# One fused transformer layer: who multiplies the Mamba sums by their gate, and when the experts' rows are added

## The reference, cut to what matters

```python
x = L0_attn_x                                   # (8, 512, 256)
xn = _layernorm(x)
x = x + attention(xn) + experts(xn)             # experts: 16, capacity 320, gathered by slot
xn = _layernorm(x)
x = x + mamba(xn) + quantised_linear(xn)

def mamba(h):                                   # 512 channels, 16 states
    x, z = split(h @ in_proj_w.T)
    u = silu(causal_conv(x) + conv1d_b)
    dt_low, B, C = split(u @ x_proj_w.T)
    delta = softplus(dt_low @ dt_proj_w.T + dt_proj_b)
    # h_t = exp(delta * A) * h_(t-1) + delta * B * u ;  y_t = sum over states of C * h_t
    y = scan(...) + u * D_param
    return (y * silu(z)) @ out_proj_w.T
```

## Time and profile before

| | |
|---|---|
| median of 3 executions | 2026.71 us (2022.96 to 2026.82) |
| the profiled execution | 2028.68 us, its span 2026.9 us |
| TensorE's mean granted clock | 0.864 |
| busy over the span: PE, DVE, ACT, POOL | 1669.0, 1511.9, 998.1, 892.4 us |
| Mix loop, first to last scan | 1075.6 to 2014.7 us |

### The profile page before, as it was taken

How to read it: one execution, slowest core, us unless ns; L and a number is a source line. 1 busy time by engine, 2 the same in 40 slices (tenths; PEclk the granted TensorE clock), 3 DMA queues, 4 the chain that set the end, 5 groups by cost and what they waited for, 6 DMA issues and landing times. The chain is left out here.

```text
span 2026.9 us, 22043 instructions
## 1 busy us (share of the span) xinstructions
PE 1669.0 (82%) x6616; PEld 747.4 (37%) x6616; DVE 1511.9 (75%) x2254; ACT 998.1 (49%) x1524; POOL 892.4 (44%) x662
## 2 busy tenths in 40 slices
PE   7388999999999999999987678687886869878465
PEld 7252534536253443526233123233332323323032
DVE  6446474564646466454658999999999999999998
ACT  3115435252533435253565756656575665657542
POOL 2710000000000000000349787978788887877863
PEclk9988989899898989999879677898877788887666
DMA  5573451536364351626234232433424233341520
GB/s 192 197 117 106 78 147 43 89 108 104 105 93 131 58 121 66 105 98 107 88 110 168 104 116 95 129 118 119 145 84 157 95 125 109 119 147 54 166 94 11
DMA packets 103331, 223.83 MB, mean 110 GB/s; under 512 B 12913, under 2 KB 65266, under 8 KB 99554
## 3 DMA queue, kind: packets, MB, share of 16 engines
q1 hardware_dynamic: 100194, 214.70, 38.2%
q0 software_dynamic: 3072, 8.37, 1.3%
HBM read 169.57 MB, written 53.48 MB: 110 GB/s over the span
## 5 line engine op out<-in xcount | busy, mean ns | idle before, releaser
L1325 POOL TENSOR_TENSOR work<-rep,bc 128x1024 f32<-128x1024 f32 x256 | 596.4, 2355 | 152.8 <-PE ps L1657 144.3
L1554 DVE TENSOR_TENSOR_SCAN ps<-ps,work 128x512 f32<-128x512 f32 x512 | 624.0, 1219 | 14.1 <-POOL work L1325 8.3
L1447 ACT ACTIVATE ps<-rep,a_neg 128x512 f32<-128x512 f32 x512 | 344.9, 688 | 294.2 <-DVE work L1560 292.2
L832 DVE TENSOR_REDUCE m<-ps 128x1 f32<-128x512 f32 x512 | 328.1, 685 | 164.0 <-PE ps L967 160.4
L719 ACT ACTIVATE prob<-ps 128x1024 f32<-128x1024 f32 x256 | 257.5, 1021 | 233.2 <-PE ps L991 231.4
L1560 DVE TENSOR_TENSOR work<-ps,bc 128x512 f32<-128x512 f32 x512 | 344.2, 672 | 0.0
L637 POOL TENSOR_TENSOR m_parts<-m,nil 128x16 bf16<-128x16 f32 x32 | 7.0, 220 | 590.0 <-DVE m L832 590.0
L1632 PE MATMUL ps<-xn_sb,front_w 128*128 128x512 f32 (+1 forms) x448 | 214.4, 632 | 33.3 <-ACT xn_sb L1381 33.3
L1657 PE MATMUL ps<-work,pick 128*32 128x512 f32 x1024 | 163.5, 717 | 83.5 <-DVE work L1560 83.5
L967 PE MATMUL ps<-k_st,q_st 96*128 96x512 bf16 x512 | 202.3, 439 | 35.6 <-DVE m L832 25.4
L991 PE MATMUL ps<-q_st,k_st 99*128 99x512 bf16 x512 | 166.5, 423 | 0.9 <-DVE e_rest L808 0.4
(11 more groups left out here) (206 smaller groups left out, 2004.2 us busy)
## 6 DMA issues: line engine op xcount, KB each, us to landing
rep<-rep_rows SPq DMA_DIRECT2D x128, 512.0 KB, 6.3
front_w<-in_w SPq DMA_DIRECT2D x32, 1024.0 KB, 8.5
bc<-bc_rows SPq DMA_DIRECT2D x32, 512.0 KB, 4.7
rep_rows<-inputs SPq DMA_DIRECT2D x32, 512.0 KB, 5.4
qk_parts<-parts SPq DMA_DIRECT2D x96, 128.0 KB
q_st<-qk_parts SPq DMA_DIRECT2D x96, 128.0 KB, 10.1
k_st<-qk_parts SPq DMA_DIRECT2D x96, 128.0 KB, 11.5
dispatch<-zeros SPq DMA_DIRECT2D x4, 1280.0 KB, 10.6
```

Source lines behind the costliest of these rows:

```text
L832: nc.vector.tensor_reduce(m[:, g % 2, qt, 2 * pair + i:2 * pair + i + 1], ps[:, S0 + i, :], AX.X, ALU.max).then_inc(s_reduced, 1)
L1325: nc.gpsimd.tensor_tensor(work[:, n % WS, :, :], rep[:, g % RS, 2 * h:2 * h + 2, 1, :], bc[:, k, 0, :].unsqueeze(1).broadcast_to([P, 2, SE ...
L1447: nc.scalar.activation(state(m), rep[:, g % RS, 2 * h + i, 0, :], ACT.Exp, scale=a_neg[:, c, 2 * h + i, k:k + 1]).then_inc(decay_ready, 1)
L1554: nc.vector.tensor_tensor_scan(state(m), state(m), work[:, n % WS, i, :], 0.0, ALU.mult, ALU.add).then_inc(state_ready, 1)
```

## The change

- On VectorE `gate_y` is left for the last sequence alone (`gate_last`). For the other 28 chunks ScalarE copies the bank into a new buffer `y_rows` (one place, `YS = 1`) behind the decays of the fifth piece of the next chunk (`take_y`, `GATE_ACT = 4`), and GpSimd multiplies it into `sz` behind its drive of 12 pieces after the chunk (`gate_y`, `GATE_POOL = 12`).
- `seed` waits for ScalarE's copy (`y_taken`), the out-projection for GpSimd's product (`gated`). ScalarE's next copy waits for the product before it.
- The weighting of the experts' rows moves from piece 21 to piece 17 on ScalarE, the addition from 26 to 24 on GpSimd, the scaling of the input from 25..28 to 26..29.

```diff
+GATE_ACT, GATE_POOL = 4, 12
+YS = 1
...
-ACT_AT = {"weigh": -11, "normalise": -3, ...
+ACT_AT = {"weigh": -15, "normalise": -3, ...
...
-POOL_AT = {"gather": -16, "add": -6, "root": -1, "down": 7, "up": 10, "input": 25}
+POOL_AT = {"gather": -16, "add": -8, "root": -1, "down": 7, "up": 10, "input": 26}
...
+        y_rows = buf("y_rows", [P, YS, SEQ])
...
+                def gate_y(b, c):
+                    pool.wait_ge(y_taken, b * DC + c + 1)
+                    if b:
+                        pool.wait_ge(sz_ready, b)
+                    else:
+                        pool.wait_ge(z_taken, DC)
+                    nc.gpsimd.tensor_tensor(sz[:, b % 2, c, :], y_rows[:, (b * DC + c) % YS, :], sz[:, b % 2, c, :], ALU.mult).then_inc(gated, 1)
...
                     drive(n // PIECES, n % PIECES)
+                    if n >= GATE_POOL + PER_CHUNK and (n - GATE_POOL) % PER_CHUNK == 0:
+                        c = (n - GATE_POOL) // PER_CHUNK - 1
+                        if c // DC < BATCH - 1:
+                            gate_y(c // DC, c % DC)
...
+                def take_y(b, c):
+                    act.wait_ge(summed, (b * PIECES + (c + 1) * PER_CHUNK) // 2)
+                    if b * DC + c >= YS:
+                        act.wait_ge(gated, b * DC + c - YS + 1)
+                    nc.scalar.activation(y_rows[:, (b * DC + c) % YS, :], ps[:, YB, :], ACT.Copy).then_inc(y_taken, 1)
...
                     decay(b, q)
+                    if n >= GATE_ACT + PER_CHUNK and (n - GATE_ACT) % PER_CHUNK == 0:
+                        c = (n - GATE_ACT) // PER_CHUNK - 1
+                        if c // DC < BATCH - 1:
+                            take_y(c // DC, c % DC)
...
-                        gate_y(c // DC, c % DC)
+                        if c // DC == BATCH - 1:
+                            gate_last(c % DC)
...
                 def seed(b, c):
-                    if c or b:
-                        pe.wait_ge(y_ready, b * DC + c)
+                    if b == BATCH - 1 and c:
+                        pe.wait_ge(y_ready, c)
+                    elif b or c:
+                        pe.wait_ge(y_taken, b * DC + c)
...
-                                pe.wait_ge(y_ready, b * DC)
+                                pe.wait_ge(gated, b * DC)
```

More of the change, by code:

```diff
@@ L72 @@
 GATE = 2
+GATE_ACT, GATE_POOL = 4, 12
+YS = 1
 PE_AT = {"turn_x": (-2, -2), "x": (0, 2, 4, 6), "turn_quant": (9, 9), "bc": 12, "dt": (14, 14, 16, 16), "z": (23, 24, 26, 27)}
-ACT_AT = {"weigh": -11, "normalise": -3, "turned": (0, 0), "x": (4, 6, 8, 10), "round": 5, "silu_u": 11, "quant": (12, 12), "rows": 14,
+ACT_AT = {"weigh": -15, "normalise": -3, "turned": (0, 0), "x": (4, 6, 8, 10), "round": 5, "silu_u": 11, "quant": (12, 12), "rows": 14,
           "dt": (16, 16, 18, 18), "softplus": 20, "z": (26, 27, 29, 30), "silu_z": 31}
 DVE_AT = {"max": 0, "statistics": -8}
-POOL_AT = {"gather": -16, "add": -6, "root": -1, "down": 7, "up": 10, "input": 25}
+POOL_AT = {"gather": -16, "add": -8, "root": -1, "down": 7, "up": 10, "input": 26}
 OUT_PROJ, OUT_COPY = (18, 19, 20, 21), (22, 24)
@@ L1172, in mix_block @@
         summed = sem("summed")
+        y_taken = sem("y_taken")
+        gated = sem("gated")
         y_ready = sem("y_ready")
@@ L1560, in read, with gate_last @@
                     nc.vector.tensor_tensor(work[:, n % WS, i, :], state(m), bc[:, k, 1, :], ALU.mult).then_inc(read_ready, 1)
-                def gate_y(b, c):
+                def gate_last(c):
+                    b = BATCH - 1
                     dve.wait_ge(summed, (b * PIECES + (c + 1) * PER_CHUNK) // 2)
[L1564 to L1567, removed]
+                    dve.wait_ge(sz_ready, b)
                     nc.vector.tensor_tensor(sz[:, b % 2, c, :], ps[:, YB, :], sz[:, b % 2, c, :], ALU.mult).then_inc(y_ready, 1)
@@ L1613, in _ @@
                 read(2 * BATCH * PIECES - 1)
-                gate_y(BATCH - 1, DC - 1)
+                gate_last(DC - 1)
             @block.tensor
@@ L1729, in _ @@
                                 pe.wait_ge(out_copied, b * HALVES)
-                            pe.wait_ge(y_ready, b * DC + 2)
+                            pe.wait_ge(y_ready, 2)
                             if t % 2 == 0:
@@ L1735, in _ @@
                         if b == BATCH - 1 and q == LAST_GATED[t]:
-                            pe.wait_ge(y_ready, b * DC + 3)
+                            pe.wait_ge(y_ready, 3)
                             out_gated(b, t, TB[t // 2], range(2, 3))
@@ L1783, in _ @@
                 sum_states(BATCH * PIECES // 2 - 1)
-                pe.wait_ge(y_ready, BATCH * DC)
+                pe.wait_ge(y_ready, DC)
                 for t in range(TT):
```

## The result

The changed kernel takes 2075.23 us (median of 4, 2072.5 to 2076.19) against 2026.03 us (median of 4, one more than in the table before the change): 2.44% slower, ratio 1.0244, interval 1.0230 to 1.0258. I had forecast 2056 us, its own range 2046 to 2066 and the wide one 2034 to 2072. The sign and the chain of waits came as forecast, the size did not: +49 us instead of +29.

What follows compares the result with a forecast made beforehand. The prediction took a loop through GpSimd's root, not VectorE, as the bound: 3.0 + 2.2 = 5.2 us a period, 26 over five, + 5 - 2.4 = +29, so 2056 us; own range 2046 to 2066, wide 2034 to 2072.

Steps and rivals of the forecast that it cites:

- the loop from A to A: Path through TensorE, ScalarE and GpSimd back to ScalarE's normalisation; claimed to set the period, 119.4 us growing to about 124.6.
- A: Moment when ScalarE's normalisation, after waiting about 3.3 us for GpSimd's shift and rstd, can start, once per period.
- The statistics' wait: VectorE's 2.2 us wait for GpSimd's experts' addition; to vanish, 11.0 us in five periods, but costed at nothing.
- GpSimd's stretch from piece 24 to A: GpSimd's nearly gapless work from the drive of piece 24 to the root; to grow by 2.2 us per period.
- The seed is 6.6 us late behind the silu: TensorE's seed of chunk 1 waits for ScalarE's copy of piece 12; GpSimd's drive of piece 16 begins 6.8 us later.
- The last gather lands 2.8 us later: Rows arrive 2.8 us after the last issue; ScalarE waits 3.2 us before weighting, delaying dt's second half 3.0 us.
- slow landing: Rival, chance 0.12: gathers fall on the rep loads and take 7.1 us, giving 2082 us; half of that, 2069.
- The sum: Total of the terms: 5.2 us a period, 26 over five, 5 before the first A, -2.4 after the last: +29.
- Gather in time: Rival, chance 0.15: weighting finds its rows, only GpSimd's 2.2 us per transition remain, +11, 2038 us.
- VectorE sets the pace: Rival, chance 0.09: A follows VectorE, so its savings of 16.8 to 28 us count; 2010 to 1999 us.
- The port lock: Rival, chance 0.04: a gate on GpSimd waits for a VectorE scan of 1.2 us; +7, 2063 us.
- No effect: Rival, chance 0.05: the late sum costs only what VectorE gave, time within 0.2%.

Runs made afterwards that it cites:

- e4: The kernel before with only the moves (weighting behind piece 17, addition behind 24, input scalings from 26), all gates on VectorE: 2030.50 us.
- e8: The kernel before with the addition behind piece 24 and the root behind GpSimd's drive of piece 29 instead of 31: 2021.25 us.
- e12: The kernel before, gates on VectorE, with the moves, the root behind piece 28 and the maxima scaled by ScalarE: 2004.00 us.
- e2: The changed kernel with ScalarE's copy one piece earlier (GATE_ACT 3), in front of the silu of u: 2043.31 us.
- e3: The changed kernel with ScalarE's copy in front of the silu and the weighting back behind piece 21: 2048.48 us.
- e6: The changed kernel with the four gathers issued behind the drives of pieces 12 and 13 instead of 16 and 17: 2046.14 us.
- e10: The changed kernel with ScalarE's copy in front of the silu and the root behind GpSimd's drive and gate of piece 28 instead of 31: 2003.00 us.
- e5: The changed kernel with the three moves taken back (weighting 21, addition 26, input scalings from 25), the gates' new path alone: 2046.94 us.
- e9: The changed kernel with half the bytes of chunk 3's rep load, which runs while the gathers land, left out: 2067.20 us.
- e11: The changed kernel with the copy in front of the silu, the root behind piece 28 and the maxima scaled by ScalarE: 1998.22 us.

## Why the forecast was right and where it failed

*The pace is set by the loop from A to A, and VectorE's savings are worth nothing.* Right. The statistics' wait went and nothing came for it (e4); in the change VectorE waits 6.89 us at piece 30 (4 to 6 forecast). With the root taken out of the way the same savings count (e8, e12: the period becomes VectorE's own work).

*GpSimd's stretch from piece 24 to A is 38.0 us instead of 35.8.* Right: 1445.85 - 1407.81 = 38.0. It is 38.1 in e2, e3 and e6 too, where it is what remains, with a drive of piece 24 that comes 0.7 to 1.3 us later than before; with the root moved out of it (e10) the loss is gone.

*The seed is 6.6 us late behind the silu.* Right in its cause (e2), and nearly in size. In the period shown it is 7.4 us late; the other 0.8 us are TensorE's start on x, eight matmuls in 6.51 us instead of 5.68. In three of the five periods they take 5.7 to 5.8 us and the seed starts 55.7 to 55.8 us after A, as forecast. Over the five it is 7.05 us late in the mean.

*The last gather lands 2.8 us later.* This is the step that failed, a term mis-sized: the rows came 6.45 us after the last issue (6.0 in the mean of five). ScalarE waited 5.3 us, not 3.2, although it reached piece 17 2.1 us later than before, which I had not counted; dt's second half slipped by 7.2 us (6.3 in the mean) instead of 3.0. I took the median of 24 gathers, although the slide by 6.8 us put the last two of each four behind the issue of the load of chunk 3. I had named that as a rival ("slow landing"), gave it 0.12, and ended the range just above its half case. That case, 2069 us, and the full one, 2082, enclose the result. e6, e5 and e9 show the contention. The warning stood in the trace of before: the one gather that took 7.1 us is the only one there that was issued just behind a load of rep, by 0.6 us (1128.64 and 1128.06), and the last of the four, which decides, took 3.1 to 4.4 us in the five other sequences.

*The sum.* In the period shown: seed and its start 0.8 more than forecast, landing 3.6 more, and 1.0 less because the out-projection and seed of piece 18 went faster once begun (8.67 us from its start to the drive of piece 24 instead of 9.70). That is about 3.2 more, 8.4 against 5.2. In the mean of the five it is 3.05 more a period, 8.25 against 5.2: 0.5 from the late issue, 3.2 from the landing, and some 0.5 less behind it. Before the first A it is 7.1 instead of 5, after the last -0.9 instead of -2.4.

*The rivals.* "Gather in time" is e2 and e6: 2043 and 2046, not 2038, because piece 24 comes at A + 84.3 and A + 84.9 there instead of A + 83.6. "VectorE sets the pace" is out for this kernel (e4). The port lock on the gates is out: GpSimd's gates took 1.25 to 1.28 us. Another instruction shows it, though, already in the trace of before (the last section). "No effect" is out.

## What to carry to other kernels

Before moving work off the busiest engine, find the loop that returns to itself once per period and price the move in it: here VectorE's savings, 28 us by the forecast, were worth nothing until GpSimd's root stood three pieces earlier, and then two changed numbers turned +2.4% into -1.2%. A step that others wait for must not stand behind a long step in its engine's queue; one piece earlier (e2) was worth 32 us. And when a transfer slides in time, price it by what it will then run beside, and by the one transfer that is waited for, not by the median of all of them where they ran before.

## What the hardware showed that I had not expected

**A small VectorE instruction held for a whole GpSimd instruction.** A tensor_scalar of 128x32 f32 within SBUF took 0.18 us in six of seven cases before and after the change, where GpSimd had just run out of drives (before: 1318.01, in a gap from 1315.75 to 1320.61). In the first sequence it took 1.91 and 1.57 us, beside drives. In e8 it took 2.31 to 2.34 us in six of seven cases (1.71 in the first) and ended with GpSimd's drive; in e10 1.05 to 1.85 us. Scans, products and the reciprocal beside the same drives kept their times. That fits the exclusive lock of the Trainium skill ("SBUF — State Buffer", who interferes with whom), which lists tensor_scalar among the instructions that can take both ports. I had expected it at the gates, where it isn't; whether it strikes is decided by the phase between two engines, which an unrelated move shifts. Scaling on ScalarE took 0.31 us and was worth 4.8 us in all (e11 against e10).

**A gather's landing about doubles beside a replicating load:** 2.7 to 2.9 us in all 24 gathers of e6, away from the loads; 5.7 to 6.3 us for two gathers of e5, issued 2.6 and 3.9 us behind the first part of one; 5.4 to 6.5 us from the last issue to the weighting in the change. The waits fell from 5.3 to 3.0 us when half of the load's bytes were left out.

**TensorE's clock after a pause, and a difference that stays open.** The seed and sum took 2.07 and 1.94 us after 6.44 us of waiting, at a granted clock of 0.50 (1.2 GHz), against 1.07 and 1.06 at 1.00 before. The first eight matmuls of x took 5.6 to 5.7 us before and 5.7 to 6.6 us in the change. In the periods shown the granted clock stayed at 0.50 for their first 5.7 us in the change and for their first 4.0 us before. The longer pause at A doesn't explain it: in e5 TensorE had paused 3.12 us there, less than before (3.79), and the same eight took 6.30 us.
